# A decoder layer on one core: VectorE's order in attention, unread products, one transposing load and the last batch by row tiles

## The chip, the core and the metric

The kernel runs on one core of one Trainium2 chip. The metric is the device time of one execution in microseconds; the kernel before takes 2635.33 us, median of 3 runs (2635.15 to 2637.47).

## What is computed

One decoder layer on 16 batches of 512 tokens with 512 channels, all in fp32: three sublayers, each added to (or multiplied with) its input and normalised over the channels.

```python
qkv = x @ Wqkv.T;  q, k = elu(q) + 1, elu(k) + 1         # 16 heads of 32 channels
running_kv, running_ksum = scan(k * v), scan(k)          # out[t] = decay * out[t-1] + in[t]
out = q * running_kv / clip(sum(q * running_ksum), 1e-6)
g = sigmoid(out @ Wgate.T + bgate)
x = layernorm(x + (g * out + (1 - g) * v) @ Wout.T)

r_t = 0.9 * r_(t-1) + ctx_t * ctx_t                      # ctx as keys and values, a scan over the tokens of the swapped axes
x = layernorm(x + x * r)

x = act_qdq(x)                                           # rounding to 16 bits, one scale for the whole tensor
up, gate = act_qdq(x @ W4(w_up).T), act_qdq(x @ W4(w_gate).T)      # W4: 4-bit weights in blocks of 32
gate = act_qdq(gate * fixed_qdq_u16(sigmoid(gate)))
x = layernorm(x + act_qdq(gate * up) @ W4(w_down).T)
```

## The kernel before

Each engine has a program of its own, written out in order by hand; engines meet at semaphores, and a wait stands in front of the instruction that needs it. Every matrix product is three: each fp32 operand is split in a high and a low part (`xh`, `xl`; `hi`, `lo`; ScalarE copies the high part, VectorE subtracts for the low one), and TensorE adds high x high, high x low and low x high, four contraction tiles deep (12 products of 512 columns for a 128 x 512 output).

**Attention phase (0 to about 1002 us).** One step per batch `s`, with a front (projections of batch `s`, scans, denominators, quotient) and a back (gate, output projection, the two normalisations of batch `s - 1`); step 0 has only a front, step 16 only a back. On TensorE the step is `qkv(s, 0)`, `gate(s)`, `qkv(s, 1 to 3)`, `project` in four row tiles j (L973), in whose second and fourth the small products `denominators` (L990) and `turn_reciprocals` (L996) are put, and `broadcast` (L1003), which reads `rec_turned`. `project` j >= 2 waits for VectorE's `first_residual` j - 2, since two banks take turns. Step 0 has no projection; there `unread` (L1005) issues products that nobody reads.

VectorE's `step` (L718) ends a front with: product 3, split of x tiles 0 and 1 of the next batch (L575), `local_sums` over the context squares (L646), a rounding of a weight piece in 12 of the steps, `first_residual` 1 (L638), `reciprocals` (L679 to L685), `first_residual` 2, split of x tiles 2 and 3, `last_sum_low`, `first_residual` 3, `quotient`. ScalarE's order beside it: x tiles 0 and 1 (L386), squares of residual rows 0 and 1, `csq_h` (L458, waits for the local sums), x tiles 2 and 3, `rec_turned` (L463), squares 2 and 3. SyncE loads x tiles 2 and 3 (L239) into the buffers `xt_raw` that the split of tiles 0 and 1 frees.

At launch `qkv(0, 0)` waits for all four splits of x and for the first of four weight splits (L543). At the end of the phase `turn_rows` (L1034) transposes the first rows of batch 0 into banks 0 to 3.

**Feed-forward phase.** After a barrier GpSimd reduces the largest magnitude, VectorE makes the scale, ScalarE rounds the first rows from banks (`first_ints` L1483, `first_high` L1487), VectorE makes the low parts (L1680), and TensorE's `step(0, 0, first=True)` waits for all four. 16 gate steps follow, then 16 up steps, 12 output tiles each over six banks (`out_ps`); ScalarE copies each tile out (L1499). Rows of the next step are rounded, stored, and brought back by a transposing load `turn` (L1240) into `q16`, from which ScalarE's `high` (L1493) and VectorE's `low` (L1680) take the parts. The first up step needs the whole gate maximum: SyncE loads the stored gate chunks (`load_gate`, L1272), ScalarE rounds them and takes the sigmoid, GpSimd rounds that (`sr_ready`), VectorE multiplies (`gated`, L1711). In `up_step` (L1274) SyncE issues the turn of the next step only after `sr_ready` of the first chunk. ScalarE's program has `high` of the next step ahead of the copies of the second group.

Then a search for the largest product, and 16 down steps: TensorE fills four row tiles (`part_used`), VectorE adds them to the residual (`sums`, L1915), takes statistics (L1918) and the variance, GpSimd the root (L1452), VectorE the bias (L1925), ScalarE normalises four tiles (L1633) and issues one store (L1636). For the last batch this chain runs behind the last product.

Of the kernel before, what the change touches and what calls it, by code (L numbers as in the profile page):

```python
# [15 lines left out]
P = 128  # L16
# [84 lines left out]
def attention_phase(nc, xT, x, ctx_in, b_gate, decay_in, w_qkv, w_go, w_ffn, w_quant, x2_dram, amax_x2, wide_h, wide_l, pairs):  # L101
# [3 lines left out]
    with ExitStack() as ctx:  # L105
# [128 lines left out]
        with nc.Block() as block:  # L234
# [303 lines left out]
            def _(dve):  # L538
# [179 lines left out]
                def step(s, par, front, back, nxt, due=True, piece=None):  # L718
# [48 lines left out]
                    if front:  # L767
                        front_values(s, 3)
                        front_product(s, 3)
                    if nxt:  # L770
                        split_x(s + 1, (0, 1))
                    if front:
                        local_sums(s + 1, 1 - par)
                    if piece is not None and 0 <= piece < NPIECE:
                        piece_rounded(piece)
                    if back:
                        first_residual(s, 1)
                    if front:
                        reciprocals(s)
                    if back:  # L780
                        first_residual(s, 2)
# [146 lines left out]
            def _(pe):  # L928
                def product(out, stat, mov, between=None):


                    n = len(stat)
                    for k in range(n):
                        (sh, sl_), (mh, ml) = stat[k], mov[k]
                        pe.matmul(out, sh, mh, start=(k == 0), stop=False)  # L935
                        pe.matmul(out, sh, ml, start=False, stop=False)  # L936
                        if between:
                            between(k)
                        mm = pe.matmul(out, sl_, mh, start=False, stop=(k == n - 1))  # L939
                    return mm  # L940
# [9 lines left out]
                def qkv(b, c):  # L950
# [3 lines left out]
                    if c == 0:  # L954
                        pe.wait_ge(xl_ready, KC * (b + 1))


# [3 lines left out]
                    product(qk_ps[c % 2][:, 0], w_tile(0, c), x_halves)  # L961
# [136 lines left out]
def ffn_phase(nc, x2_dram, w_ffn, w_ffn_t, q_dram, up_dram, gate_dram, gs_dram, amax_x2, wide_h, wide_l, pairs, out):  # L1098
# [4 lines left out]
    with ExitStack() as ctx:  # L1103
# [114 lines left out]
        with nc.Block() as block:  # L1218
            @block.sync
            def _(sp):  # L1220
# [53 lines left out]
                def up_step(b, par, ahead):  # L1274
                    for g in range(NG):
                        t = NG * b + g
                        if ahead:
                            if g == 0:
                                turn_free(NB + b + 1, 1 - par, 16 * (NB // 2))
                            sp.wait_ge(sr_ready, t + 1)  # L1280
                            load_gate(b + 1, g)
                            if g == 0:
                                turn(b + 1, 1 - par)
# [29 lines left out]
                for g in range(NG):  # L1313
                    load_gate(0, g)
                up_step(0, 0, True)
# [74 lines left out]
                for u in range(2):  # L1390
                    sp.wait_ge(d_stored[u], 16 * (NB // 2))

            @block.gpsimd
            def _(pool):
# [72 lines left out]
                root(NB - 1)  # L1467

            @block.scalar
            def _(act):  # L1470
# [11 lines left out]
                def first_ints(k):  # L1482
                    act.activation(q16[:, 0, k], banks[k], ACT.Copy, scale=inv_x).then_inc(ints_ready, 1)  # L1483
# [184 lines left out]
                normalise(NB - 1, 1)  # L1668

            @block.vector  # L1670
            def _(dve):
# [250 lines left out]

                def norm_bias(b):
# [28 lines left out]
                sums(NB - 1, 1, NB // 2 - 1)  # L1952
                norm_bias(NB - 1)

            @block.tensor
            def _(pe):
                def tile(s, par, m, first):
                    if not (first and m < 6):
                        pe.wait_ge(evacuated, MT * s + m - 5)
                    for k in range(KC):  # L1960
                        o = out_ps[m % 6][:]
# [13 lines left out]
                def step(s, par, weights=None, first=False, new=None):  # L1975
                    pe.wait_ge(lo_ready, KC * (s + 1))
# [7 lines left out]
                    if new is not None:  # L1984
                        turn(new, (2, 3))
                step(0, 0, first=True)
# [94 lines left out]
```

## Time and profile before

The profiled execution took 2635.85 us; its span on the core is 2633.7 us.

| | busy us | share of the span |
|---|---|---|
| TensorE products | 2533.0 | 96% |
| VectorE | 2019.5 | 77% |
| ScalarE | 1355.5 | 51% |
| GpSimd | 389.3 | 15% |

The mean granted TensorE clock is 0.986 of full speed. The phases in the span: attention to about 1002 us, gate 1009 to 1577, up to 2072, the search to 2110, down to 2621, the last stores to the end. The chain that ended last lies mostly on TensorE (57% of the span, by what the profile follows). Where TensorE is busy without a gap, other engines' idle time costs nothing; so its gaps are read first, then who is late at each.

### The profile page before, as it was taken

To read this page: it belongs to the slowest core of one execution; us is meant where nothing else is said; L and a number is where in the kernel's file an instruction comes from. 1 tells how busy PE (TensorE), PEld (TensorE's weight loads), DVE (VectorE), ACT (ScalarE), POOL (GpSimd) and SP (SyncE) were. 2 spreads that over 40 slices of the span, in tenths; PEclk is the share of its full clock that TensorE was granted. 3 is DMA by queue.
4 is the path that set the end of the run, shared out by engine and by line. 5 is a ranking of instruction groups with operands and counts; after the bars stand their busy time and mean duration, and the time that the engine had idled before them with its cause. 6 is when DMAs were issued, how large, how long until landed. Compare 5 with 4: busy or idle time off the path is not lost.

```text
span 2633.7 us, 31986 instructions
## 1 busy us (share of the span) xinstructions
PE 2533.0 (96%) x11190; PEld 2117.6 (80%) x11190; DVE 2019.5 (77%) x2820; ACT 1355.5 (51%) x1727; POOL 389.3 (15%) x278
## 2 busy tenths in 40 slices
PE   7999999999999997999999999999999699999998
PEld 5888888888888886888888878888888588888886
DVE  7899999999999994555555459987777766666664
ACT  4455555555565654333333358888888522222222
POOL 0000000000000000000000003322222133333331
PEclk9999999999999998999999999999999899999999
DMA  4011222121111225555555458877777635555552
GB/s 176 9 64 72 95 108 76 72 80 72 72 72 68 102 110 176 188 183 186 185 183 184 167 192 295 288 259 258 255 255 255 261 146 221 211 211 211 211 211 92
DMA packets 146282, 429.85 MB, mean 163 GB/s; under 512 B 73136, under 2 KB 81584, under 8 KB 106416
## 3 DMA queue, kind: packets, MB, share of 16 engines
q1 hardware_dynamic: 143920, 412.39, 43.2%
q10 hardware_dynamic: 2304, 16.78, 1.5%
q8 instruction: 25, 0.41, 0.1%
q14 instruction: 33, 0.27, 0.0%
HBM read 235.67 MB, written 177.21 MB: 157 GB/s over the span
## 4 chain that ended last, share of the span: by engine, by line
PE 57%; issue 1%; DVE 1%; DMA 1%; ACT 1%; POOL 0%; SPq 0%; POOLq 0%; DVEq 0%; ACTq 0%
PE pair L1962 13%; PE pair L1963 13%; PE pair L1964 13%; PE pair L2014 6%; PE pair L2016 6%; PE pair L2015 6%; PE pair L1972 0%; DMA ff_gs<-gate_ints 0%; DMA ff_q<-x_ints 0%; DVE ff_sr L1884 0%; DMA up_products<-ff_group 0%; ACT ff_group L1499 0%; ACT ff_group L1633 0%; DVE ff_stats L1918 0%; DVE ff_group L1915 0%
## 5 line engine op out<-in xcount | busy, mean ns | idle before, releaser
L1962 PE MATMUL pair<-ff_hi,wide_h 128*128 128x512 f32 x1536 | 600.5, 391 | 17.7 <-DVE ff_lo L1680 13.9
L1964 PE MATMUL pair<-ff_hi,wide_l 128*128 128x512 f32 x1536 | 599.2, 390 | 0.0
L1963 PE MATMUL pair<-ff_lo,wide_h 128*128 128x512 f32 x1536 | 598.9, 390 | 0.0
L1499 ACT ACTIVATE ff_group<-pair,ff_scales 128x512 f32<-128x512 f32 x384 | 257.4, 686 | 303.8 <-PE pair L1964 293.4
L1962 PEld LDWEIGHTS pair<-ff_hi,wide_h 128*128 128x128 f32 x1536 | 289.3, 188 | 78.4 <-DVE ff_lo L1680 14.3
L1964 PEld LDWEIGHTS pair<-ff_hi,wide_l 128*128 128x128 f32 x1536 | 289.1, 188 | 60.3
L1963 PEld LDWEIGHTS pair<-ff_lo,wide_h 128*128 128x128 f32 x1536 | 289.4, 188 | 59.7
L2014 PE MATMUL pair<-wide_h,ff_hi 128*128 128x512 f32 x768 | 299.6, 390 | 25.0 <-DVE ff_lo L1900 23.4
L935 PE MATMUL pair<-xh,wide_h 128*128 128x512 f32 x768 | 302.1, 393 | 12.7 <-DVE xl L575 12.7
L936 PE MATMUL pair<-xl,wide_h 128*128 128x512 f32 x768 | 300.3, 391 | 0.0
L939 PE MATMUL pair<-xh,wide_l 128*128 128x512 f32 x768 | 300.2, 391 | 0.0
L2016 PE MATMUL pair<-wide_h,ff_lo 128*128 128x512 f32 x768 | 299.3, 390 | 0.0
L2015 PE MATMUL pair<-wide_l,ff_hi 128*128 128x512 f32 x768 | 299.2, 390 | 0.0
L1692 DVE TENSOR_REDUCE ff_gate_max<-ff_group 128x2048 f32 (+1 forms) x48 | 109.7, 2286 | 213.1 <-ACT ff_group L1499 213.1
L1654 ACT ACTIVATE ff_hi<-ff_sr 128x2048 fp32r<-128x2048 int16 x47 | 90.2, 1918 | 338.3 <-PE pair L2016 326.3
L1906 DVE TENSOR_TENSOR ff_lo<-ff_sr,ff_hi 128x2048 fp32r<-128x2048 int16 x47 | 107.6, 2289 | 135.6 <-ACT ff_hi L1654 135.6
L2014 PEld LDWEIGHTS pair<-wide_h,ff_hi 128*128 128x128 f32 x768 | 144.6, 188 | 55.7 <-issue 23.8
L349 POOL TENSOR_TENSOR rstd<-var_eps,mhalf 128x4 f32<-128x4 f32 x30 | 48.1, 1604 | 920.8 <-DVE var_eps L627 920.8
L935 PEld LDWEIGHTS pair<-xh,wide_h 128*128 128x128 f32 x768 | 145.1, 189 | 46.3 <-issue 16.5
L939 PEld LDWEIGHTS pair<-xh,wide_l 128*128 128x128 f32 x768 | 145.0, 189 | 30.4
L936 PEld LDWEIGHTS pair<-xl,wide_h 128*128 128x128 f32 x768 | 145.0, 189 | 29.8
L2015 PEld LDWEIGHTS pair<-wide_l,ff_hi 128*128 128x128 f32 x768 | 144.6, 188 | 30.1
(228 smaller groups left out, 4603.5 us busy)
## 6 DMA issues: line engine op xcount, KB each, us to landing
gate_products<-ff_group SPq DMA_DIRECT2D x48, 1024.0 KB, 4.0
ff_raw<-gate_products SPq DMA_DIRECT2D x48, 1024.0 KB, 5.7
up_products<-ff_group SPq DMA_DIRECT2D x48, 1024.0 KB, 4.3
ff_raw<-up_products SPq DMA_DIRECT2D x48, 1024.0 KB, 9.2
gate_ints<-ff_gs SPq DMA_DIRECT2D x48, 512.0 KB, 2.7
ff_gs<-gate_ints SPq DMA_DIRECT2D x48, 512.0 KB, 9.9
xt_raw<-in_xT SPq DMA_DIRECT2D x64, 256.0 KB, 3.4
csq<-in_ctx_rows SPq DMA_DIRECT2D x16, 1024.0 KB, 7.3
```

The lines of the kernel that those rows point to most:

```text
L935: pe.matmul(out, sh, mh, start=(k == 0), stop=False)
L936: pe.matmul(out, sh, ml, start=False, stop=False)
L939: mm = pe.matmul(out, sl_, mh, start=False, stop=(k == n - 1))
L1499: act.activation(group[:, g, m * T:(m + 1) * T], out_ps[(GM * g + m) % 6][:], ACT.Copy, scale=s_x).then_inc(evacuated, 1)
L1692: dve.tensor_reduce(gate_max[:, 0, bass.ds(t, 1)], group[:, g], AX.X, ALU.max).then_inc(gate_max_ready, 1)
L1906: dve.tensor_tensor(flat(lo[:, sl]), o16[:, sl].bitcast(I16), flat(hi[:, sl]).bitcast(F32), ALU.subtract).then_inc(ol_ready, 1)
L1962: pe.matmul(o, wh[:, m, k], hi[:, par, k], start=(k == 0), stop=False)
L1963: pe.matmul(o, wh[:, m, k], lo[:, par, k], start=False, stop=False)
L1964: mm = pe.matmul(o, wl[:, m, k], hi[:, par, k], start=False, stop=(k == KC - 1))
L2014: pe.matmul(o, hi[:, sl, k, rows], mh, start=(g == 0 and k == 0), stop=False)
L2015: pe.matmul(o, hi[:, sl, k, rows], ml, start=False, stop=False)
L2016: mm = pe.matmul(o, lo[:, sl, k, rows], mh, start=False, stop=(g == NG - 1 and k == KC - 1))
```

## The change

- VectorE in an attention step: `first_residual` 1 and `reciprocals` go ahead of the split of x tiles 0 and 1; `first_residual` 2 ahead of the rounding of the weight piece.
- TensorE at launch waits for the x splits one by one, inside the first product; in step 0 `unread` issues 20 and 20 products in place of 14 and 6.
- `turn_rows` and `first_ints` use banks 2, 3, 0, 1 in place of 0 to 3; TensorE's feed-forward part begins with 8 unread products into the last bank, and its first tile waits for the low parts one by one.
- SyncE: the turn of the second up step is issued behind the third of the first gate loads, its own waits ahead of that load; the first `up_step` leaves it out.
- The last batch of the down part: sum, statistics, variance, root, bias, normalisation and store go row tile by row tile.

```diff
@@ VectorE, attention step
                     if front:
                         front_values(s, 3)
                         front_product(s, 3)
+                    if back:
+                        first_residual(s, 1)
+                    if front:
+                        reciprocals(s)
                     if nxt:
                         split_x(s + 1, (0, 1))
                     if front:
                         local_sums(s + 1, 1 - par)
+                    if back:
+                        first_residual(s, 2)
                     if piece is not None and 0 <= piece < NPIECE:
                         piece_rounded(piece)
-                    if back:
-                        first_residual(s, 1)
-                    if front:
-                        reciprocals(s)
-                    if back:
-                        first_residual(s, 2)
                     if nxt:
                         split_x(s + 1, (2, 3))
@@ TensorE, attention
+                        if ahead:
+                            ahead(k)
...
-                    if c == 0:
+                    first = isinstance(b, int) and n == 0
+                    if c == 0 and not first:
                         pe.wait_ge(xl_ready, KC * (b + 1))
...
-                    product(qk_ps[c % 2][:, 0], w_tile(0, c), x_halves)
+                    product(qk_ps[c % 2][:, 0], w_tile(0, c), x_halves,
+                            ahead=(lambda k: pe.wait_ge(xl_ready, k + 1)) if first else None)
...
-                            mm = pe.transpose(turn_banks[k][:, j * P:(j + 1) * P], first_rows[:, j, k * P:(k + 1) * P], ident_f)
+                            mm = pe.transpose(turn_banks[(k + 2) % KC][:, j * P:(j + 1) * P], first_rows[:, j, k * P:(k + 1) * P], ident_f)
...
-                        unread(14)
+                        unread(20)
                         denominators(s)
-                        unread(6)
+                        unread(20)
                         turn_reciprocals(s)
@@ SyncE, up
-                            if g == 0:
+                            if g == 0 and turns:
                                 turn_free(NB + b + 1, 1 - par, 16 * (NB // 2))
...
                 for g in range(NG):
+                    if g == NG - 1:
+                        turn_free(NB + 1, 1, 16 * (NB // 2))
                     load_gate(0, g)
-                up_step(0, 0, True)
+                turn(1, 1)
+                up_step(0, 0, True, turns=False)
@@ GpSimd, last batch
-                root(NB - 1)
+                for j in range(TT):
+                    pool.wait_ge(ve_ready, NB + j)
+                    pool.tensor_tensor(rstd[:, j:j + 1], var_eps[:, j:j + 1], mhalf[:, j:j + 1], ALU.pow).then_inc(rstd_ready, 1)
@@ ScalarE, last batch
-                normalise(NB - 1, 1)
+                for j in range(TT):
+                    cols = slice(j * HID, (j + 1) * HID)
+                    act.wait_ge(nmr_ready, NB + j)
+                    act.activation(x2_res[:, 1, cols], x2_res[:, 1, cols], ACT.Identity, scale=rstd[:, j:j + 1],
+                                   bias=nmr[:, j:j + 1]).then_inc(norm_ready, 1)
+                    act.wait_ge(norm_ready, TT * (NB - 1) + j + 1)
+                    act.dma_start(out[NB - 1][:, j], x2_res[:, 1, cols]).then_inc(d_stored[1], 16)
@@ VectorE, last batch
+                def last_sums():
+                    dve.wait_ge(d_x2_in[1], 16 * (NB // 2))
+                    for j in range(TT):
+                        n = TT * (NB - 1) + j + 1
+                        cols, row = slice(j * HID, (j + 1) * HID), slice(j, j + 1)
+                        dve.wait_ge(part_used, TT * (NG * NB - 1) + j + 1)
+                        dve.scalar_tensor_tensor(x2_res[:, 1, cols], banks[TT + j][:], s_o, x2_res[:, 1, cols],
+                                                 ALU.mult, ALU.add).then_inc(sum_ready, 1)
+                        if j > 0:
+                            last_bias(j - 1)
+                        dve.wait_ge(sum_ready, n)
+                        dve.bn_stats(stats[:, j], x2_res[:, 1, cols]).then_inc(stats_ready, 1)
...
+                    last_bias(TT - 1)
@@ TensorE, feed-forward
+                        if first and m == 0:
+                            pe.wait_ge(lo_ready, k + 1)
...
-                    pe.wait_ge(lo_ready, KC * (s + 1))
+                    if not first:
+                        pe.wait_ge(lo_ready, KC * (s + 1))
...
+                unread(8)
                 step(0, 0, first=True)
```

## Rows read from the trace of the kernel before

**Rows 1.** TensorE's instruction groups: busy, mean ns | idle before them, by releaser
```profile
L1962 PE MATMUL pair<-ff_hi,wide_h 128*128 128x512 f32 x1536 | 600.5, 391 | 17.7 <-DVE ff_lo L1680 13.9 <-ACT ff_group L1499 3.8
L935 PE MATMUL pair<-xh,wide_h 128*128 128x512 f32 x768 | 302.1, 393 | 12.7 <-DVE xl L575 12.7
L935 PE MATMUL pair<-go_h,ah 128*128 128x512 f32 x256 | 105.8, 413 | 21.0 <-DVE xrow L638 19.3 <-DVE al L856 1.4 <-DVE csq L816 0.3
```
**Rows 2.** Timeline of VectorE in one attention step: start us, us, engine, line, what
```profile
528.85 1.29 DVE L575 TENSOR_TENSOR xl<-xt_raw,xh 128x512 fp32r<-128x512 f32 x2
530.05 2.14 DVE L646 SCALAR_TENSOR_TENSOR csq<-csq 128x512 f32<-128x512 f32 x3
...
532.57 0.68 DVE L638 SCALAR_TENSOR_TENSOR xrow<-pair,xrow 128x512 f32<-128x512 f32 x1
...
534.57 0.68 DVE L638 SCALAR_TENSOR_TENSOR xrow<-pair,xrow 128x512 f32<-128x512 f32 x1
```
**Rows 3.** Timeline of TensorE in the same step
```profile
528.67 0.40 PE L939 MATMUL pair<-go_h,al 128*128 128x512 f32 x1
...
533.31 0.62 PE L935 MATMUL pair<-go_h,ah 128*128 128x512 f32 x1 [1.42 <-DVE xrow L638]
...
536.88 0.49 PE L1003 MATMUL pair<-rec_turned,head_bc 32*128 32x512 f32 x1
```
**Rows 4.** Timeline of ScalarE in the same step
```profile
534.20 0.62 ACT L458 ACTIVATE csq_h<-csq 128x512 fp32r<-128x512 f32 x1
...
535.76 0.57 ACT L463 ACTIVATE rec_turned<-pair 32x512 fp32r<-32x512 f32 x1
```
**Rows 5.** Windows: us, busy PE, PEld, DVE, ACT, POOL, granted clock, DMA share, GB/s
```profile
533.30:592.70 59.40, 57.97 (x257) 49.40 (x257) 57.60 (x104) 34.04 (x55) 3.24 (x2) 1.00 0.21 80
...
60.00:64.40 4.40, 4.40 (x11) 3.19 (x11) 3.80 (x7) 2.42 (x4) 0.00 (x0) 0.50 0.86 327
...
1008.70:1013.30 4.60, 4.56 (x11) 3.59 (x12) 0.00 (x0) 1.36 (x1) 0.00 (x0) 0.50 0.53 150
...
1576.50:1579.90 3.40, 3.40 (x10) 2.65 (x9) 3.40 (x2) 3.40 (x3) 0.00 (x0) 0.50 0.64 265
```
**Rows 6.** Timeline of VectorE, TensorE and ScalarE, launch and step 0
```profile
9.60 1.76 DVE L543 TENSOR_TENSOR wide_l<-first_chunks,wide_h 128x1536 fp32r<-128x1536 f32 x1 [4.18 <-ACT wide_h L371]
...
52.02 1.06 PE L990 MATMUL pair<-head_sum,qks 128*128 128x16 f32 x8 [1.41 <-DVE qks L600]
...
57.12 0.63 ACT L458 ACTIVATE csq_h<-csq 128x512 fp32r<-128x512 f32 x1 [8.00 <-DVE csq L646]
```
**Rows 7.** Timeline of VectorE, low parts of the first feed-forward rows
```profile
1005.28 0.69 DVE L1680 TENSOR_TENSOR ff_lo<-ff_q,ff_hi 128x512 fp32r<-128x512 int16 x1 [1.93 <-ACT ff_hi L1487]
...
1007.39 1.29 DVE L1680 TENSOR_TENSOR ff_lo<-ff_q,ff_hi 128x512 fp32r<-128x512 int16 x2 [0.40 <-ACT ff_hi L1487]
```
**Rows 8.** Timeline of SyncE and ScalarE, gate to up; landings of ff_q's transposing loads
```profile
1565.52 4.96 SPq L1240 DMA_TRANSPOSE ff_q<-x_ints  x1
...
1572.53 2.19 ACT L1493 ACTIVATE ff_hi<-ff_q 128x512 fp32r<-128x512 int16 x4 [8.29 <-DMA ff_q<-x_ints]
...
DMA to landing us min/median/max: 6.5/7.0/13.0
```
**Rows 9.** Roots on one and on four columns (ns min/median/max); ScalarE's last timeline row
```profile
L362 POOL TENSOR_TENSOR rstd<-var_eps,mhalf x8: 539/543/549, 981.3 to 994.7; 128x1 f32<-128x1 f32 x8
...
L1452 POOL TENSOR_TENSOR ff_rstd<-ff_var_eps,ff_mhalf x16: 1007/1008/3150, 2142.7 to 2624.0; 128x4 f32<-128x4 f32 x16
...
2625.21 2.93 ACT L1633 ACTIVATE ff_group<-ff_group,ff_nmr,ff_rstd 128x512 f32<-128x512 f32 x4 [18.08 <-DVE ff_nmr L1925]
```
**Rows 10.** DMA issues: out<-in, queue, count, KB each, median us to landing
```profile
xt_raw<-in_xT SPq DMA_DIRECT2D x64, 256.0 KB, 3.4
...
out_rows<-ff_group ACTq DMA_DIRECT2D x16, 1024.0 KB, 3.9
...
x_rows<-csq SPq DMA_DIRECT2D x4, 256.0 KB, 2.4
```

More of the change, by code:

```diff
@@ L928, in _, with product @@
             def _(pe):
-                def product(out, stat, mov, between=None):
+                def product(out, stat, mov, between=None, ahead=None):
                     n = len(stat)
                     for k in range(n):
+                        if ahead:
+                            ahead(k)
                         (sh, sl_), (mh, ml) = stat[k], mov[k]
@@ L1272, in load_gate, with up_step @@
                     sp.dma_start(raw[:, g], gate_dram[NG * b + g]).then_inc(raw_in[g], 16)
-                def up_step(b, par, ahead):
+                def up_step(b, par, ahead, turns=True):
                     for g in range(NG):
@@ L1281, in up_step @@
                             load_gate(b + 1, g)
-                            if g == 0:
+                            if g == 0 and turns:
                                 turn(b + 1, 1 - par)
@@ L1389, in _ @@
                 down_loads(NB - 1, 1, NB // 2 - 1, False)
-                for u in range(2):
-                    sp.wait_ge(d_stored[u], 16 * (NB // 2))
+                sp.wait_ge(d_stored[0], 16 * (NB // 2))
+                sp.wait_ge(d_stored[1], 16 * (NB // 2 - 1 + TT))
             @block.gpsimd
@@ L1482, in first_ints @@
                 def first_ints(k):
-                    act.activation(q16[:, 0, k], banks[k], ACT.Copy, scale=inv_x).then_inc(ints_ready, 1)
+                    act.activation(q16[:, 0, k], banks[(k + 2) % KC], ACT.Copy, scale=inv_x).then_inc(ints_ready, 1)
                 def first_high(k):
@@ L1921, in sums, with last_bias @@
                     row_moments(dve, stats, msum[:], mdiff[:], msq[:], var_eps[:], moments_ready, square_ready, ve_ready, b + 1)
+                def last_bias(j):
+                    row = slice(j, j + 1)
+                    dve.wait_ge(rstd_ready, NB + j)
+                    dve.scalar_tensor_tensor(nmr[:, row], msum[:, row], -0.5, rstd[:, row], ALU.mult, ALU.mult).then_inc(nmr_ready, 1)
+                def last_sums():
[10 more added lines that the diff above has]
+                        dve.bn_stats(stats[:, j], x2_res[:, 1, cols]).then_inc(stats_ready, 1)
+                        if j == 0:
+                            dve.wait_ge(norm_ready, TT * (NB - 1))
+                        dve.wait_ge(stats_ready, n)
+                        row_moments(dve, stats[:, row], msum[:, row], mdiff[:, row], msq[:, row], var_eps[:, row],
+                                    moments_ready, square_ready, ve_ready, NB + j)
+                    last_bias(TT - 1)
                 def norm_bias(b):
@@ L1951, in _ @@
                 norm_bias(NB - 2)
-                sums(NB - 1, 1, NB // 2 - 1)
-                norm_bias(NB - 1)
+                last_sums()
             @block.tensor
@@ L1985, in step, with unread @@
                         turn(new, (2, 3))
+                def unread(n):
+                    for _ in range(n):
+                        pe.matmul(out_ps[5], wide_h[:, 0:P], wide_h[:, 0:T], start=True, stop=True)
+                unread(8)
                 step(0, 0, first=True)
```

## The prediction

> **What bounds the kernel now.** Start with TensorE's groups of instructions, whose last column says what it idled for [rows 1]: of the waits there this change touches four, 19.3 us for VectorE's residual rows in attention (14 times, up to 1.42), 13.9 us at the first product of the feed-forward part, 12.7 us at the launch and 3.8 us at the turn from gate to up. Everywhere else TensorE is fed, so time comes off only where such a wait, or the lower clock behind it, goes. Then ask of each wait what is late next. For the 14 waits read one step engine by engine: VectorE [rows 2], TensorE [rows 3], ScalarE [rows 4], and the windows [rows 5], which say that in a 59.4 us step VectorE is busy 57.6 us. Little can come out of such a step. Last, the single places: launch and step 0 [rows 6], first feed-forward products [rows 7], the turn [rows 8], the end [rows 9] and how long stores take to land [rows 10].
>
> **VectorE's order in attention.** Nothing is removed; the second residual tile and the reciprocals (2.00 us together, from L638 at 532.57 to the next L638 at 534.57 [rows 2]) go ahead of the split of two x tiles (1.20 us, 528.85 to 530.05) and the local sums (530.05 to 532.22, 2.17 us). The stall goes: residual 1 would be ready near 529.9, before the third projection is through. But follow what is late next. First, residual 1 needs projection 1, whose last product starts at 528.67 and takes 0.40 us [rows 3], so it starts at 529.10 and VectorE idles 0.25 us. Second, the local sums now end at 529.10 + 2.00 + 1.20 + 2.17 = 534.47, 2.25 us later. On ScalarE the copy csq_h waits for them, then two x splits, then the copy of the turned reciprocals: from csq_h's start (534.20) to the end of that copy (535.76 + 0.57 = 536.33) is 2.13 us [rows 4]. After the change that is 534.50 + 2.13 = 536.63, and the broadcast product, which reads it, starts at about 536.66 instead of 536.88. So the wait moves from ahead of the fourth projection to ahead of the broadcast, and a step gains 0.22 us, not 1.42. It repeats: broadcast, 52 us of products to projection 1, 5.4 us of VectorE, 2.1 us of ScalarE make 59.2 us, against 59.4. VectorE's own round, without its idle time for ScalarE, is about 59.0, so two limits lie close together. Thirteen periods x 0.21 = 2.8, with 0.3 for the first and last step: **3.1 us**. Bounds: the split that now comes later also frees xt_raw later (531.7 and 532.3), and SyncE's two loads of the next x tiles are behind it; by the landings of 256 KB moves, 2.4 us for one and 3.4 at the median of the x loads [rows 10], they land between 534.1 and 535.7, against ScalarE's need at 535.0 and 535.5. If the median holds, the gain is gone, and a little more: -1 us. The other bound is VectorE's round, 0.43 a step, 5.6 us.
>
> **Launch and step 0.** The first product waited for all four x splits, until 12.7. The low half of the first weights ends at 9.60 + 1.76 = 11.36 [rows 6] and the first x tiles are there by then, so it starts 1.3 us sooner. But the first products run at the lower clock, and the time at which it rises need not move with them; of the 1.3 between nothing and all may be left, I carry 0.7. In step 0 the unread products grow from 14 + 6 to 20 + 20. Back to back products take 0.227 us each (257 in 57.97 [rows 5], small ones among them), 20 of them 4.5 us. The first batch ends as its denominators get ready (the idle 1.41 us behind it goes), the second before the broadcast can start: reciprocals come sooner, but csq_h, which waited 8.00 us for the local sums until 57.12 [rows 6], comes 1.2 us later by VectorE's order, and behind it the 2.1 us of ScalarE [rows 4]. So the broadcast starts near 57.1 - 0.7 + 1.2 + 2.1 = 59.7, against 60.0, and a new gap of about 2 us is in front of it. Of the clock, the windows show 0.50 from 60.0 to 64.4 [rows 5], 2.2 us lost, most of it in step 1's first products; ahead of its fall lay 1.41 us idle and 8 products of 16 columns [rows 6]. The longer unread runs fill that gap, but the new one may take the clock down in its turn, for 1.7 of the 2.2. I take 0.4 for the order and 0.7 for the clock, **1.1**. Bounds: -0.3 (nothing from launch or clock, and the 1.2 only just covered) and 2.8.
>
> **Feed-forward start.** The first x2 tile's low part is done at 1005.28 + 0.69 = 1005.97, the last at 1007.39 + 1.29 = 1008.68 [rows 7]; the first product waited for the last. It now begins behind the first, 2.7 us sooner, and may run each k as its tile comes. Eight unread products (8 x 0.43 = 3.4 us, from about 1002.6) lie wholly in the idle time; their cover is 13.9 us wide and costs nothing. They also start the clock's rise: in the profile TensorE ran 1008.7 to 1013.3 at 0.50 [rows 5], which cost 4.6 / 2 = 2.3 us. If it rises near 1007.7, the first tile's 12 products are held by the low parts and end at about 1009.6 instead of 1013.7. Bounds: 2.7 (the clock rises as late in the work as before) and 4.3; **4.0**. The other order of banks only makes bank 2 the one that is read first; it costs nothing.
>
> **Up's turn.** SyncE issued the transposing load of the next rows only after GpSimd's first rounding, at 1565.5; ScalarE stood 8.29 us in front of its copy ff_hi, from 1564.24, and began it at 1572.53, with the copies out of PSUM queued behind it [rows 8]; TensorE ran out of banks, 3.8 us [rows 1], and then 1576.5 to 1579.9 at 0.50 [rows 5], 1.7 us. Now the turn is issued right behind the three gate loads, about 1550.6. Landing takes 6.5 to 13.0 us [rows 8]: 1563.5 at the worst, and ScalarE reaches the copy at 1564.24. TensorE needs it only by about 1568.8 (2.1 us of copies and one copy out of PSUM before 1571.5). What SyncE is moved past: the turn's issue (5 us of its queue) falls into a stretch in which it waited anyway, and its stores of the first up chunk come 1.3 us sooner. No next wait within 5 us on any engine: low parts are done near 1571.7, needed at 1577. Sum 3.8 + 1.7 + 0.2 for a product started cold = **5.7**; the lower bound is 3.8, should the clock fall all the same. By the Trainium skill (DMA: Bandwidth & Descriptors, Queues, rings and completion order) an engine takes descriptors in ring order, so the turn's data can't start before the gate loads' are through. That speaks against this edit; with 3 MB ahead it puts landing near 1562.5, still early enough, and the sum stays.
>
> **The last batch.** From the last sum to the variance nothing shrinks. Then the root on one column takes 0.54 instead of 1.01, the four normalisations (2.93 us) become one of 0.80, and the store is issued at about 2625.6 instead of 2628.2 [rows 9]. The store has 256 KB: four such stores landed in 2.4 us, the 1 MB ones in 3.9 [rows 10]. Sum 2.5 + 1.5 = **4.0**; bounds 3.3 and 4.3. The rows of tiles 0 to 2 hide under TensorE, which gives a tile every 2.72 us against about 2.4 us of VectorE, bias included. By the Trainium skill (DMA: Bandwidth & Descriptors, Anatomy of one DMA: about 2.0 us plus bytes over 436 GB/s) the store would take an estimated 2.6 us, and the sum would be 3.8; the row decides.
>
> **Sum.** 1.1 + 3.1 + 4.0 + 5.7 + 4.0 = 17.9 us. Against the profiled execution's 2635.85 that is 2618.0, against the median of the runs (2635.33), 0.5 lower, 2617.4; I forecast 2617.5. All gains stay, since TensorE is busy without a gap behind each place. Lowest values together: -0.3 - 1 + 2.7 + 3.8 + 3.3 = 8.5, 2627.3. Highest: 2.8 + 5.6 + 4.3 + 5.9 + 4.3 = 22.9, 2612.9.
>
> **Rivals.** (1) *The new gap lowers the clock in some steps.* Ahead of the broadcast TensorE will idle about as long as before the fourth projection (1.42 us), with small products near it. Against: with 1.42 us idle the step's window stays at 1.00 [rows 5]. For: 1.41 us idle beside small products did bring it down in step 0. Each fall costs a stretch like 1576.5 to 1579.9, 1.7 us. In a third of the steps: +7.5, 2625. Chance 0.13. (2) *The x loads land late* and the steps gain nothing: 2617.5 + 3.1 + 0.5 = 2621.1. Chance 0.10. (3) *The stall is simply gone*: 19.3 instead of 3.1, 2601.3. Against it stands VectorE, busy 57.6 of 59.4. Chance 0.04. (4) *Slower*: the same fall as in (1), at every broadcast: 14 x 1.7 = 23.8, 2641.3. It decides from 11 falls on (17.9 / 1.7). Chance 0.02. (5) *The turn does not come sooner for ScalarE* (its packets wait, or GpSimd's first rounding slips by them): 2617.5 + 5.7 = 2623.2. Chance 0.04. The forecast has 0.67.
>
> **Range and chances.** 0.2% is 5.3 us, about what a measurement of this kernel can tell from no change. The forecast, (1), (2), (3) and (5) lie below 2630. The range takes the bounds of the sum, and with them (1), (2) and (5): 2612.5 to 2627. Faster 0.94, same 0.03 (more falls than (1), or several low ends at once), slower 0.03.
>
> **What would show it.** Right: no wait of TensorE for xrow in attention, in its place one of 1.4 to 1.7 us before the broadcast (L1003's product) for ScalarE's rec_turned, steps of 59.2 us; the first feed-forward product about 3.5 us behind the memset that opens the part; no wait of TensorE between 1550 and 1600 and clock 1.00 there; four normalisations 2.7 us apart and the end about 4 us closer to the last product. Wrong: steps of 59.4 with ScalarE waiting for xt_raw (2), windows at 0.50 in steps (1, 4), steps under 58.9 (3).

## The result and the profile after

The changed kernel takes 2640.31 us (median of 20 runs, 2638.02 to 2643.91) against 2635.20 (20 runs): ratio 1.0019, 95% interval 1.0012 to 1.0026. It is slower by 5 us where 17.8 less were forecast. Its profiled execution took 2641.53 us with a span of 2639.8 (before 2635.85 and 2633.7), at a mean granted clock of 0.983 (0.986).

TensorE's groups, the lines that answer to [rows 1]:

```profile
L1999 PE MATMUL pair<-ff_hi,wide_h 128*128 128x512 f32 x1536 | 599.7, 390 | 3.0 <-ACT ff_group L1504 2.8
L935 PE MATMUL pair<-xh,wide_h 128*128 128x512 f32 x768 | 309.2, 403 | 12.3 <-DVE wide_l L543 11.7
...
L935 PE MATMUL pair<-go_h,ah 128*128 128x512 f32 x256 | 102.3, 400 | 1.7 <-DVE al L856 1.4 <-DVE csq L816 0.3
...
L1003 PE MATMUL pair<-rec_turned,head_bc 32*128 32x512 f32 x16 | 7.9, 492 | 24.2 <-ACT rec_turned L463 24.2
```

The 19.3 us for `xrow` are gone, and 24.2 us stand in front of the broadcast, for ScalarE: the forecast's new wait. The 13.9 us at the first feed-forward product have gone too (eight unread products fill them, below). Now one step, engine by engine; TensorE, then VectorE, then ScalarE (start, length, line, idle time before):

```profile
542.40 0.39 PE L939 MATMUL pair<-go_h,al 128*128 128x512 f32 x1
544.38 0.49 PE L1003 MATMUL pair<-rec_turned,head_bc 32*128 32x512 f32 x1 [1.58 <-ACT rec_turned L463]
544.96 0.49 PE L935 MATMUL pair<-xh,wide_h 128*128 128x512 f32 x1
```
```profile
536.78 0.69 DVE L638 SCALAR_TENSOR_TENSOR xrow<-pair,xrow 128x512 f32<-128x512 f32 x1 [0.17 <-PE pair L939]
...
538.80 1.29 DVE L575 TENSOR_TENSOR xl<-xt_raw,xh 128x512 fp32r<-128x512 f32 x2
540.00 2.14 DVE L646 SCALAR_TENSOR_TENSOR csq<-csq 128x512 f32<-128x512 f32 x3
```
```profile
542.18 0.63 ACT L458 ACTIVATE csq_h<-csq 128x512 fp32r<-128x512 f32 x1 [3.65 <-DVE csq L646]
542.71 1.14 ACT L386 ACTIVATE xh<-xt_raw 128x512 fp32r<-128x512 f32 x2
543.75 0.57 ACT L463 ACTIVATE rec_turned<-pair 32x512 fp32r<-32x512 f32 x1
```

Residual 1 to the end of the local sums is 5.4 us, `csq_h` to the end of the copy 2.14, as worked out in advance. What was not in the sum shows in TensorE's windows (length, busy time, granted clock, DMA share, GB/s). The second is a step from broadcast to broadcast without a fall of the clock, the third a step with one, the last is in the up part:

```profile
123.16:126.57 3.41, 3.41 (x9) 0.50 0.00 0
182.12:241.52 59.40, 57.68 (x257) 1.00 0.21 80
302.32:363.33 61.01, 59.29 (x257) 0.97 0.21 77
1618.20:1621.61 3.41, 3.41 (x9) 0.50 0.85 327
```

Stretches of 3.41 us at 0.50 (1.2 GHz) begin 1.0 to 2.0 us behind the broadcast in 10 of the 14 steps from 123.16 to 908.23, and one at 61.72 behind step 0; the kernel before has none of these. (One more, behind the last broadcast, is in both: 955.28 before, 969.67 after.) Such a stretch is called a fall below. A step with a fall takes 60.8 to 61.0 us, a step without one 59.2 or 59.4, so a fall costs 1.6.

Five marks split the difference: the memset that opens the feed-forward part, the last gate store, the last up store, the last product, the end. Of before, GpSimd, SyncE twice and TensorE:

```profile
1002.53 0.10 POOL L1395 MEMSET ff_mhalf<- 128x4 f32 x1 [1.36 <-POOLq L107]
1545.08 0.33 SPq L1261 DMA_DIRECT2D gate_products<-ff_group  x1
2073.06 0.33 SPq L1287 DMA_DIRECT2D up_products<-ff_group  x1
2621.18 0.39 PE L2016 MATMUL pair<-wide_h,ff_lo 128*128 128x512 f32 x1
```

Of after:

```profile
1017.59 0.10 POOL L1398 MEMSET ff_mhalf<- 128x4 f32 x1 [1.36 <-POOLq L107]
1556.07 0.33 SPq L1261 DMA_DIRECT2D gate_products<-ff_group  x1
2083.01 0.33 SPq L1287 DMA_DIRECT2D up_products<-ff_group  x1
2630.91 0.39 PE L2060 MATMUL pair<-wide_h,ff_lo 128*128 128x512 f32 x1
```

| stretch | before | after | difference | forecast |
|---|---|---|---|---|
| start to memset | 1002.53 | 1017.59 | +15.06 | -4.2 |
| to the last gate store | 542.55 | 538.48 | -4.07 | -4.0 |
| to the last up store | 527.98 | 526.94 | -1.04 | -5.7 |
| to the last product | 548.12 | 547.90 | -0.22 | 0 |
| to the end of the span | 12.52 | 8.89 | -3.63 | -4.0 |

The feed-forward start and the last batch held; attention and up's turn did not. In up, SyncE's transposing loads and ScalarE's copies of them, after:

```profile
1561.38 9.14 SPq L1240 DMA_TRANSPOSE ff_q<-x_ints  x1
...
1603.14 9.89 SPq L1240 DMA_TRANSPOSE ff_q<-x_ints  x1
```
```profile
1575.12 2.18 ACT L1498 ACTIVATE ff_hi<-ff_q 128x512 fp32r<-128x512 int16 x4
...
1615.16 2.19 ACT L1498 ACTIVATE ff_hi<-ff_q 128x512 fp32r<-128x512 int16 x4 [10.09 <-DMA ff_q<-x_ints]
```

The first copy no longer waits. The second waits 10.09 us, TensorE runs out of banks for 2.8, and the clock falls at 1618.20. The kernel before shows the same wait, with TensorE too far behind to feel it:

```profile
1606.26 2.19 ACT L1493 ACTIVATE ff_hi<-ff_q 128x512 fp32r<-128x512 int16 x4 [7.34 <-DMA ff_q<-x_ints]
```

### The profile page after: what moved, and what is told of

It reads as the page before. It is cut to its first block, busy times and chain, and to the rows that moved or that the text cites. A ratio compares the mean times of both kernels' runs of the same rounds, so it can differ in the third digit from the quotient of the medians.

```text
span 2639.8 us, 32066 instructions
## 1 busy us (share of the span) xinstructions
PE 2550.7 (97%) x11218; PEld 2132.8 (81%) x11218; DVE 2020.0 (77%) x2838; ACT 1356.8 (51%) x1727; POOL 397.1 (15%) x281
## 4 chain that ended last, share of the span: by engine, by line
PE 57%; DVE 2%; DMA 1%; ACT 1%; issue 1%; SPq 0%; POOL 0%; POOLq 0%; ACTq 0%; DVEq 0%
PE pair L1999 12%; PE pair L2001 12%; PE pair L2000 12%; PE pair L2058 6%; PE pair L2059 6%; PE pair L2060 6%; DMA ff_q<-x_ints 0%; PE pair L2009 0%; DVE ff_gs L1722 0%; DMA ff_gs<-gate_ints 0%; DMA up_products<-ff_group 0%; DVE ff_up_max L1745 0%; DVE ff_up_abs L1727 0%; DVE ff_lo L1917 0%; ACT ff_group L1504 0%
## 5 line engine op out<-in xcount | busy, mean ns | idle before, releaser
L2001 PEld LDWEIGHTS pair<-ff_hi,wide_l 128*128 128x128 f32 x1536 | 288.7, 188 | 60.4
L2000 PEld LDWEIGHTS pair<-ff_lo,wide_h 128*128 128x128 f32 x1536 | 288.7, 188 | 59.4
L935 PE MATMUL pair<-xh,wide_h 128*128 128x512 f32 x768 | 309.2, 403 | 12.3 <-DVE wide_l L543 11.7
L939 PE MATMUL pair<-xh,wide_l 128*128 128x512 f32 x768 | 307.0, 400 | 0.0
L936 PE MATMUL pair<-xl,wide_h 128*128 128x512 f32 x768 | 306.7, 399 | 0.0
L2060 PEld LDWEIGHTS pair<-wide_h,ff_lo 128*128 128x128 f32 x768 | 144.6, 188 | 30.2
```

The source lines that it names most:

```text
L2000: pe.matmul(o, wh[:, m, k], lo[:, par, k], start=False, stop=False)
L2001: mm = pe.matmul(o, wl[:, m, k], hi[:, par, k], start=False, stop=(k == KC - 1))
L2060: mm = pe.matmul(o, lo[:, sl, k, rows], mh, start=False, stop=(g == NG - 1 and k == KC - 1))
```

## The experiments

Theory after the result: the new idle time ahead of the broadcast takes the clock down, and the falls are the loss in attention; the second turn takes up's gain. Where several edits act, the marks above are used.

**Which part.** `order_back` is the changed kernel with VectorE's order of before, `order_alone` the kernel before with the new order only (its edit, abridged as all edits below; `order_back` is the same, reversed):

```diff
+first_residual(s, 1); reciprocals(s)
 split_x(s + 1, (0, 1)); local_sums(s + 1, 1 - par)
+first_residual(s, 2)
 piece_rounded(piece)
-first_residual(s, 1); reciprocals(s); first_residual(s, 2)
```

> The changed kernel with VectorE's attention order as it was before the change; all other parts stay. Theory (clock): the attention phase lost 15 us because TensorE's clock fell behind the new 1.58 us wait before the broadcast in 10 steps, and everything else there is about -1. So the 10 low stretches of 3.41 us go, the phase is back at 1 us under the kernel before, and the time is 2640.3 - 16 = 2624. Rival (launch): the falls come from step 0's longer unread runs or the earlier start, which shift where in the work the clock is looked at. Then most of the falls stay and the time is 2638 to 2641.

> The kernel before with VectorE's new attention order alone. Theory (clock): about 10 falls of the clock behind the broadcast's wait, at 1.6 us each, less 0.2 us a step for the order: 2635.2 + 16 - 3 = 2648, within 2645 to 2652. Rival (launch): no falls, 2632. Rival (order as forecast, the low stretches are harmless): 2632.

Measured: 2622.36 us, ratio to the kernel before 0.9945 (0.9932 to 0.9959), no fall in a step, memset at 999.34; and 2650.36, 1.0055 (1.0041 to 1.0069), 10 falls in steps, memset at 1018.27. The order alone costs 14 us (`order_alone` against the kernel before) to 18 us (the changed kernel against `order_back`), and without it the rest of the change is a gain. (Where the expectations count 10 low stretches in the changed kernel, it is 10 in steps and the one behind step 0.)

**The order or the clock.** `fill` keeps the order and gives TensorE work in the wait:

```diff
+pe.wait_ge(phi_ready, KC * (s + 1))
+for _ in range(7):
+    pe.matmul(bc_bank, qkv_h[:, 0, 0, 0:P], qkv_h[:, 0, 0], start=True, stop=True)
 pe.wait_ge(rec_turned_ready, s + 1)
-pe.wait_ge(phi_ready, KC * (s + 1))
```

> The changed kernel with 7 unread products of 512 columns (7 x 0.227 = 1.6 us) ahead of each broadcast, into the bank that the broadcast overwrites, in front of its wait for ScalarE. TensorE's wait for ScalarE stays, but the engine is not idle in it. Theory (clock): the low stretches in the steps go, every step takes 59.2 us, and the time is 2640.3 - 10 x 1.6 = 2624. Rival (order): VectorE's and ScalarE's order costs the time and the clock only goes along with it: no change, 2640.

Measured: 2622.07 us, 0.9946 (0.9933 to 0.9960). Fourteen steps of each, in TensorE's windows; of the changed kernel, of `order_back` and of `fill`:

```profile
122.00:965.00 843.00, 821.71 (x3580) 0.98 0.21 79
```
```profile
119.00:947.00 828.00, 809.82 (x3580) 1.00 0.22 81
```
```profile
118.00:947.00 829.00, 828.33 (x3681) 1.00 0.21 81
```

VectorE and ScalarE work in the same order as in the changed kernel, and the 18 us are back. So it is the clock, not the order. Second reading, what the order itself is worth: the broadcasts of steps 1 and 15 start 829.7 us apart before (121.1, 950.8) and in `order_back`, 829.8 in `fill`, and 828.8 with two products (`fill_2`, below). Behind these sums, 12 of the 14 steps of before take 59.4 us and the last two 59.1 and 57.9. In `fill_2` steps of 59.2 and of 59.35 to 59.5 take turns, and the last takes 58.0; in `fill` seven products overfill the wait of the last step, which takes 59.1. So the new order brings 0.1 us a step, about 1 us in all; the forecast had taken the 59.2 for every step.

**Moving the wait.** `copy_first` puts ScalarE's copy `rec_turned` ahead of `csq_h`; `copy_first_k` moreover waits for x tiles one by one:

```diff
 if front:
+    act.wait_ge(turned_ready, s + 1)
+    act.activation(rec_turned[:], turn_bank, ACT.Copy).then_inc(rec_turned_ready, 1)
     act.wait_ge(summed, (TT - 1) * (s + 1))
...
-    act.wait_ge(turned_ready, s + 1)
-    act.activation(rec_turned[:], turn_bank, ACT.Copy).then_inc(rec_turned_ready, 1)
@@ copy_first_k alone
-if c == 0 and not first:
-    pe.wait_ge(xl_ready, KC * (b + 1))
-        ahead=(lambda k: pe.wait_ge(xl_ready, k + 1)) if first else None)
+        ahead=(lambda k: pe.wait_ge(xl_ready, KC * b + k + 1)) if c == 0 else None)
```

> The changed kernel with ScalarE's copy rec_turned ahead of csq_h and of the second pair of x splits, so that the broadcast finds it ready (near 541.6 for a need at 542.8). TensorE's next need is then the low part of the last x tile, which VectorE ends near 544.6: the wait of about 1.5 us moves behind the broadcast, in front of the next step's first product, and a step stays at 59.0 to 59.2 us. Theory (the length of the idle time alone decides on the clock): falls as before, 2640. Rival (what stands beside the idle time decides; now 512-column products on one side and one of 32 rows on the other): fewer falls; with none 2624.

> copy_first, with TensorE waiting for the x tiles of every step one by one inside the first product, so that the last low part is needed 2.1 us later in it. Theory (length): the wait of 1.6 us behind the broadcast shrinks under 0.5, the falls go, and what is left is VectorE's round, 59.0 to 59.2 us: 2620 to 2623. Rival: VectorE's round makes TensorE wait as long in another place of the step, and the clock falls there: 2632 to 2636.

Measured: 2636.10 us, 1.0001 (0.9992 to 1.0010), with 9 falls; and 2611.01, 0.9905 (0.9890 to 0.9920), with none. What TensorE waited for in 14 steps of `copy_first`, then of `copy_first_k` (sum, times, longest):

```profile
PE pair L934 <- DVE xl L574: 22.1, 14, 1.6
```
```profile
PE pair L934 <- DVE att L701: 11.4, 14, 1.1
```

As expected the wait moved behind the broadcast and the clock kept falling; the time is 4 us under the 2640 expected. With the tiles needed later, no wait is left there, TensorE waits 0.8 us a step ahead of the gate products instead, and the clock stays in all 14 steps. The time of `copy_first_k` is 9 us under what I expected: a step comes to 58.7 us where I had taken VectorE to hold it at 59.0 to 59.2, and the way from broadcast 0 to 1 takes 57.6 where it takes 59.3 in `fill`.

**How long, and beside what.** `fill_1` and `fill_2` are `fill` with one and two products. `gap_longer` and `gap_2us` are the kernel before with one and three more small operations on VectorE ahead of residual 1 (of the first, without its conditions):

```diff
+dve.wait_ge(den_ready, s + 1)
+dve.tensor_scalar(den_rec[:], den_bank, 1e-6, None, ALU.max).then_inc(again, 1)
 first_residual(s, 1)
```

> The changed kernel with one unread product ahead of each broadcast instead of seven: about 1.36 us of TensorE's wait before the broadcast stay idle, as much as the 1.42 us that stood ahead of the fourth projection in the kernel before without a fall. Theory (length): between 1.4 and 1.6 us of idle time the clock begins to fall, so here it stays: 2624, as with seven. Rival (what stands beside the gap): the small products around the broadcast count with it, so most of the falls stay: 2636 to 2640.

> The kernel before with one more small operation of VectorE (the maximum over the denominators, written once more, about 0.25 us) ahead of residual 1, so that TensorE idles 1.6 to 1.7 us ahead of the fourth projection instead of 1.42, among products of 512 columns. Each step is 0.2 us longer, +3 us without a fall. Theory (length of the idle time): the clock falls in about 10 steps as it did at 1.58 us before the broadcast, 2635.5 + 3 + 16 = 2654. Rival (what stands beside the gap): at this place the clock stays, 2638 to 2640.

> The changed kernel with two unread products ahead of each broadcast: about 1.13 us stay idle, 1.7 us with the broadcast behind it. Theory (length, seen with its neighbours): under what held at the fourth projection, so no fall in the steps: 2622 to 2624. Rival (small products beside any gap of a microsecond do it): 2 or more falls, 2625 to 2630.

> As gap_longer, with three of the small operations ahead of residual 1 in place of one: TensorE idles about 2.0 us ahead of the fourth projection, each step is 0.6 us longer than in the kernel before, +8 without a fall. Theory (length, seen with its neighbours): ahead of the broadcast the dense products stand apart by 1.58 us idle and the broadcast of 32 rows, whose successor starts 0.58 us behind it: 2.2 us in all, with one unread product 2.0 (3 falls in 14 steps). At the fourth projection nothing stands beside the gap, 1.51 us held the clock, and 2.0 should take it down in some steps: 2646 to 2660. Rival (the place, whatever the length): no fall, 2643 to 2645.

Measured: `fill_1` 2628.43 us, 0.9976 (0.9965 to 0.9986); `gap_longer` 2639.21, 1.0014 (1.0005 to 1.0023); `fill_2` 2620.05, 0.9942 (0.9929 to 0.9956); `gap_2us` 2667.44, 1.0119 (1.0104 to 1.0135). TensorE around the gap, for `fill_1`, `gap_longer` and `gap_2us`:

```profile
535.86 0.40 PE L1003 MATMUL pair<-wide_h 128*128 128x512 f32 x1
537.61 0.49 PE L1005 MATMUL pair<-rec_turned,head_bc 32*128 32x512 f32 x1 [1.35 <-ACT rec_turned L463]
538.20 0.49 PE L935 MATMUL pair<-xh,wide_h 128*128 128x512 f32 x1
```
```profile
533.89 0.40 PE L943 MATMUL pair<-go_h,al 128*128 128x512 f32 x1
535.85 0.62 PE L939 MATMUL pair<-go_h,ah 128*128 128x512 f32 x1 [1.56 <-DVE xrow L639]
```
```profile
547.13 0.40 PE L948 MATMUL pair<-go_h,al 128*128 128x512 f32 x1
549.72 0.81 PE L944 MATMUL pair<-go_h,ah 128*128 128x512 f32 x1 [2.20 <-DVE xrow L639]
```

By the idle time alone the runs contradict each other: 3 falls at 1.35 us, none at 1.56. `fill_1` also lies between its two expectations. Take instead the time from the start of the last full product (128 rows, 512 columns) to the start of the next, so that the broadcast with 32 rows counts to the gap. With the gap ahead of the broadcast, most second steps have about 0.2 us more of it, so two values stand there; run by run they fall in line:

| kernel | gap | idle us | start to start us | falls in 14 steps |
|---|---|---|---|---|
| before | fourth projection | 1.42 | 1.82 (first and last 1.49) | 0 |
| `gap_longer` | fourth projection | 1.56 | 1.96 (1.62) | 0 |
| `fill_2` | broadcast | 1.12 | 1.95, 2.11 to 2.19 | 0 |
| `fill_1` | broadcast | 1.35 | 2.17, 2.34 | 3 (all at 2.34) |
| `copy_first` | behind the broadcast | 1.59 | 2.38 to 2.40 | 9 |
| after | broadcast | 1.58 | 2.39, 2.56 to 2.61 | 10 (6 of 8, 4 of 6) |
| `gap_2us` | fourth projection | 2.20 | 2.60 (2.25, 2.44) | 14 |

So the first theory, the idle time alone, fell with `gap_longer`, and its rival, the place, fell with `gap_2us`. There the time is above the range given, because the clock fell in all 14 steps: the mean step is 61.3 us, 0.4 for the longer wait and 1.6 for the clock over the mean of before, 59.3. `fill_2` came out as the theory had it, 2 us better. The order of the rows is measured; that the 32-row product counts little because of its rows is only argued, since no run changed its rows alone.

The length of one gap does not settle what that gap does. In the changed kernel a gap of 2.59 held (step 2) and gaps of 2.39 did not; in `gap_2us` one of 2.25 took the clock down, and in its up part one of 3.83 (3.44 idle) did not:

```profile
1602.57 0.39 PE L1973 MATMUL pair<-ff_hi,wide_l 128*128 128x512 f32 x1
1606.40 0.50 PE L1971 MATMUL pair<-ff_hi,wide_h 128*128 128x512 f32 x1 [3.44 <-ACT ff_group L1508]
```
```profile
1602.57:1609.00 6.43, 2.99 (x13) 1.00 1.04 369
```

In the changed kernel the falls come later behind the broadcast from one step to the next (1.00, 1.44 and 2.04 us in steps 6 to 8), and the step after that has none. That fits a part that the moment of a gap plays beside its length, but no run moved the moment alone, and it stays open.

**Up's turn.** `turn_alone` is the kernel before with that part of the change; `turns_early` is `fill` with every turn a step sooner:

```diff
-if g == 0 and turns:
-    turn_free(NB + b + 1, 1 - par, 16 * (NB // 2))
 sp.wait_ge(sr_ready, t + 1)
 load_gate(b + 1, g)
-if g == 0 and turns:
-    turn(b + 1, 1 - par)
+if g == 2 and turns:
+    turn_free(NB + b + 2, par, 16 * (NB // 2))
+    turn(b + 2, par)
```

> The kernel before with the earlier first turn of the up part alone. The forecast said 5.7 us. Theory now: the first stall (3.8 us) and its low clock (1.7) go, and a stall of 1.9 to 2.8 us comes at the second turn, with or without a fall of the clock: a gain of 1.0 to 3.6 us, 2632 to 2635. Rival (the forecast as it stands, its loss in the changed kernel is due to the clock's phase): 5.7, 2630.

> The changed kernel with seven unread products before the broadcast, and with every transposing load of the up part one step sooner: the turn of step b + 2 is issued behind the third gate load of step b (its buffer is free since the low parts of step b are made). The changed kernel issued the second of them at 1603.14, and ScalarE waited 10.09 us for it, TensorE 2.8. Theory (the stall moved to the next turn, because that one still hangs on the gated chunks): no TensorE wait between the gate's end and the last up store, 1 to 3 us less than with the seven products alone (2622.1): 2620. Rival (the transposing loads delay SyncE's other work and GpSimd, and that is what holds ScalarE): the same or slower, 2622 to 2626.

Measured: 2634.16 us, 0.9994 (0.9985 to 1.0003), which by itself is not clear of no change, with TensorE waiting 2.7 us at the second turn and a low stretch at 1604.33; and 2620.31, 0.9941 (0.9927 to 0.9955). From last gate store to last up store `turn_alone` takes 526.88 us, 1.1 less than before, `fill` 523.59 (a wait of 1.1 us at the second turn and no fall; the waits of 1.9 and 2.0 in `order_back` and `copy_first_k` brought none either), and `turns_early`, where neither ScalarE nor TensorE waits, 522.23: 5.75 less than before. That is the forecast's 5.7, once both turns are early.

**Launch and the other two parts.**

> The kernel before with the launch's single waits and step 0's longer unread runs alone. With VectorE's order taken back, the attention phase ended 3.2 us sooner than in the kernel before, against 1.1 forecast for the launch and step 0 with the new order. Theory: the low stretch of 10.24 us in step 0 goes, and with the product that starts sooner it is 3.2 us: 2633. Rival (the forecast's 1.1 or less, the rest is a fall at 955 us that comes and goes): 2635.

> The kernel before with the feed-forward start and the last batch by row tiles alone. The forecast had 4.0 + 4.0 = 8.0 us for them; the traces' marks give 3.8 to 4.1 for the start and 3.6 for the end: 2635.5 - 7.6 = 2628. Rival (a gap turns up behind the sooner start): 2631 or more.

Measured: 2631.34 us, 0.9984 (0.9975 to 0.9993), memset at 998.56, 4.0 sooner than before; and 2628.28, 0.9972 (0.9961 to 0.9982), 7.6 less where the forecast's terms had 8.0. Step 0 of `launch_alone`:

```profile
51.42 4.79 PE L1012 MATMUL pair<-wide_h 128*128 128x512 f32 x20
56.97 0.42 PE L1000 MATMUL pair<-ident_r,rec_halves 128*32 128x128 f32 x4 [0.75 <-DVE rec_halves L685]
57.23 0.68 PE L1012 MATMUL pair<-wide_h 128*128 128x512 f32 x2
58.07 0.49 PE L1007 MATMUL pair<-rec_turned,head_bc 32*128 32x512 f32 x1 [0.16 <-ACT rec_turned L463]
```

The clock does not fall here at all. In the changed kernel 2.00 us stand in front of that broadcast, which starts at 60.4, and the clock falls behind it.

**Putting it together.** `best` is `order_back` with the turns of `turns_early`; `best2` is `copy_first_k` with them.

> The changed kernel with VectorE's attention order as before and every transposing load of the up part one step sooner; no unread products in the attention steps. order_back gave 2622.4 with TensorE waiting 1.9 us at the second turn. Expected 1.9 to 2.2 less: 2620.3. If seven unread products had done more than hold the clock (turns_early, 2620.3), this one is 1 us or more behind it: 2621.5.

> copy_first_k with every transposing load of the up part one step sooner. The two act in different phases: 2611.0 less the 2.0 us that TensorE waited at the second turn, 2609. Rival (a sooner attention phase makes the gate's end late for the turn): 2611.

Measured: 2618.76 us, 0.9935 (0.9921 to 0.9948); and 2608.08, 0.9892 (0.9877 to 0.9907), which beats both kernels, by 28 us against before. A step of `best2`, with TensorE, its weight loads, VectorE, ScalarE and GpSimd busy in it:

```profile
527.00:585.66 58.66, 57.90 (x258) 49.25 (x257) 57.52 (x104) 34.11 (x56) 3.24 (x2) 1.00 0.22 81
```

## Why the prediction was wrong, step by step

**VectorE's order.** The chain was right: the wait went where it was said to go, with the size said (1.4 to 1.7; it is 1.58). Two things failed. The small one is the term: 3.1 us took every step from 59.4 to 59.2. The steps of before are 59.4 but for the last two; with the new order and no fall only every second one is 59.2, the others stay near 59.4 (`fill_2`), so the order is worth about 1 us. The upper bound took VectorE's round for 59.0; the steps of `best2` are 58.7 us in the mean.

**Rival (1), the step that failed.** Its "Against" said that with 1.42 us idle the step stays at 1.00 [rows 3, 5], and took it as evidence for a gap at another place, near a product with 32 rows; the sum put the clock in the steps at nothing ("All gains stay"). Rival (4) had the mechanism and price for a slower result and got 0.02. Counted start to start, TensorE's rows of before gave a warning:

```profile
531.49 0.40 PE L939 MATMUL pair<-go_h,al 128*128 128x512 f32 x1
...
536.56 0.40 PE L939 MATMUL pair<-go_h,al 128*128 128x512 f32 x1
...
537.30 0.50 PE L935 MATMUL pair<-xh,wide_h 128*128 128x512 f32 x1
```

From 531.49 to the next full product at 533.31 [rows 3] are 1.82 us, and that held. The forecast put the broadcast at 536.66, so the product behind it at 537.1; the last one ahead of it, 536.56, comes 1.42 us sooner by the wait taken out, and 0.2 by the first product behind that wait, which had taken 0.46 in place of 0.23: near 534.9. That is a gap of about 2.2 us, not one "about as long", and it lies between the 1.82 that held and step 0's first gap, which counts 2.7 (50.23 to 52.94, with 8 products of 16 columns in it) and was followed by a fall at 54.16. It measured 2.39 to 2.61, and the clock fell 10 times: 10 x 1.6 = 16 us. What a gap of 2.2 would do the trace of before could not say. Rival (4)'s turning point was 11 falls; with the 4.7 us that up's turn didn't bring, 10 and the one of step 0 sufficed.

**Launch and step 0.** Forecast 1.1 with a bound of 2.8; alone it is 4.0. Of that I had valued the low clock at 2.2, but the low stretch of before is 10.24 us long and begins at 54.16, in step 0 itself, ahead of the window that I read [rows 5]:

```profile
54.16:64.40 10.24, 6.57 (x18) 0.50 0.72 248
```

With the new order the gain is lost again (second broadcast at 121.3, before 121.1), by the mechanism named there, a gap of 2 us ahead of the broadcast.

**Feed-forward start.** Forecast 4.0, measured 4.07. In the changed kernel's TensorE rows the unread products end as the low parts arrive, and the first product runs 3.5 us behind the memset, at full clock:

```profile
1017.63 3.57 PE L2027 MATMUL pair<-wide_h 128*128 128x512 f32 x8 [7.80 <-PEq L107]
1021.09 0.50 PE L1999 MATMUL pair<-ff_hi,wide_h 128*128 128x512 f32 x1
```

**Up's turn.** The step that failed is "No next wait within 5 us on any engine". ScalarE's 7.34 us for the second turn were in the trace of before, one step beyond the stretch that I read, and harmless there because the first stall had made room. The turn of the second step stands in SyncE's queue behind the stores of the third gated chunk (ready at 1597.89), two loads of weights (3.0 us from 1598.79) and a gate load that waits for the fourth rounded chunk, and came only 1.1 us sooner (1593.21 to 1603.14, less the 11.0 of the gate's end). Of 5.7, 2.8 went to the new wait and 1.7 to its low clock. Rival (5) had the size, 2623.2, by another cause: the first turn did land early. By the Trainium skill (DMA: Bandwidth & Descriptors, Queues, rings and completion order) an engine takes descriptors in ring order; the sum stood by that rule, with 11.9 us from issue to landing. The two turns landed 12.7 and 12.0 us behind their issue, the first behind three gate loads, the second behind one, so the runs do not show that the loads ahead set it.

**The last batch.** Forecast 4.0, measured 3.63: the last product to the end took 8.89 us, with a normalisation of 0.81 and the store behind it:

```profile
2634.39 0.81 ACT L1676 ACTIVATE ff_group<-ff_group,ff_nmr,ff_rstd 128x512 f32<-128x512 f32 x1 [1.39 <-DVE ff_nmr L1937]
2635.23 0.34 ACTq L1679 DMA_DIRECT2D out_rows<-ff_group  x1
```

From last product to issue it is 4.32 us, before 6.99: 2.7 less, where 2.5 was worked out. What follows the issue shrank by 1.0 in place of 1.5. The four stores landed in 2.5 us each. The formula of the Trainium skill in the prediction (DMA: Bandwidth & Descriptors, Anatomy of one DMA), which gave 2.6, is stated there for transfers that GpSimd issues; ScalarE issued these.

## What to carry to other kernels

When a stall of TensorE moves, price the clock at its new place: measure the gap from the last full product to the next, partial-row products counted to the gap, and compare it with gaps of the same trace that did and did not take the clock down. If it is longer than those that held in every step, count on falls in some of the steps. Two unread products in a wait that can't be removed cost nothing and were worth 20 us here. And when a stall is taken out, read the trace one step further than the stall, for waits of helpers that it had been hiding.

## What the runs showed of the hardware

In attention the clock fell at gaps of little over 2 us, in a stream that kept TensorE busy over 57 of 59 us a step: in none of 42 steps at up to 2.2 us (the kernel before, `gap_longer`, `fill_2`), in 3 of 14 at 2.17 and 2.34, in 9 and 10 of 14 at 2.38 to 2.61, in 14 of 14 in `gap_2us`, where all but two are 2.60. The low stretch in a step was 3.41 us at 1.2 GHz each time and cost 1.6. Yet 3.44 us idle in the up part of `gap_2us` left it at full speed. The Trainium skill (TensorE: Matmul & The Clock Gate, HAM oscillation — how this bites in real kernels) warns only of idle gaps longer than any in these steps, where the clock fell; the measurement decides. The section after it (A second HAM failure mode: psum-queue depth-cycling) tells of a clock that swings where TensorE idles shortly and often between groups of products; what is seen here is nearer to that, with one such gap in 59 us.

VectorE's product of gated chunks took longer in the changed kernel when GpSimd's rounding (1.9 us) was running as it started or started with it: 4.14 us at 1576.88, 3.57 at 1594.32 and 3.86 at 1602.96, against 2.34 at 1585.54. The extra 1.8, 1.2 and 1.5 us are nearly the time that both ran together (1.9, 1.4 and 1.7). The second of them is the third gated chunk, which the late turn stood behind. No run separated the two engines, so the cause stays open.
